# Attention output projection in three fp32r parts, with head outputs and weight split into high and low, and less scratch for GpSimd's DMAs

## The reference

```python
q = (x @ Wq.T + bq); k = (context @ Wk.T + bk); v = (context @ Wv.T + bv)   # to 16 heads of 32
attn = softmax(einsum('bhnd,bhmd->bhnm', q, k) * scale, axis=-1)
out = einsum('bhnm,bhmd->bhnd', attn, v)      # heads side by side again: (n, 512)
return out @ Wo.T + bo
```

## Time and profile before

| | |
|---|---|
| time, median of 3 runs | 2181.3 us (2181.11 to 2185.82) |
| profiled execution, its own time | 2182.54 us |
| its span | 2180.8 us |
| granted TensorE clock, mean | 0.965 |
| busy, share of the span | PE 92%, PEld 60%, DVE 65%, ACT 56%, POOL 18% |
| instructions | 39849 |

### The profile page before, as it was taken

One profiled execution on the slowest core, in us unless ns is written; L12 is line 12 of the kernel. 1 busy time (PEld: TensorE's weight loads), 2 busy tenths in 40 slices (PEclk: granted clock), 3 DMA queues, 4 the chain that ended last, 5 costly groups with the idle time before them and its releaser, 6 DMA issues. The chain is left out here.

```text
span 2180.8 us, 39849 instructions
## 1 busy us (share of the span) xinstructions
PE 2004.3 (92%) x13356; PEld 1317.6 (60%) x13356; DVE 1413.9 (65%) x2811; ACT 1223.4 (56%) x3068; POOL 389.6 (18%) x595
## 2 busy tenths in 40 slices
PE   4799999999999999858999999999999999689978
PEld 3576767666766676544555555555655564278843
DVE  6778786868686868526556565656565655266428
ACT  3353535353535353317878787777777777246514
POOL 1010101010101010230221212122222222100006
PEclk9899999999999999978999999999999999889989
DMA  4304040303030303232323232424342322261165
GB/s 162 84 18 118 17 119 20 117 21 113 17 115 21 114 16 98 81 120 65 110 76 112 74 113 73 118 80 117 79 117 79 102 75 69 77 218 59 58 228 216
DMA packets 117216, 200.94 MB, mean 92 GB/s; under 512 B 22944, under 2 KB 40352, under 8 KB 117024
## 3 DMA queue, kind: packets, MB, share of 16 engines
q1 hardware_dynamic: 107808, 179.46, 27.0%
q0 software_dynamic: 9216, 18.89, 3.4%
HBM read 117.53 MB, written 29.88 MB: 68 GB/s over the span
## 5 line engine op out<-in xcount | busy, mean ns | idle before, releaser
L1555 ACT ACTIVATE a_shared<-a_shared,a_mx 128x512 f32<-128x512 f32 x512 | 340.6, 668 | 51.0 <-DVE a_mx L1603 50.9
L1548 ACT ACTIVATE a_probs<-a_scores 128x512 f32<-128x512 f32 x512 | 291.7, 602 | 111.2 <-PE a_scores L1706 109.0
L1603 DVE TENSOR_REDUCE a_mx<-a_shared 128x1 f32<-128x512 f32 x512 | 318.3, 681 | 29.8 <-PE a_shared L1690 29.2
L901 PE MATMUL m_proj<-m_xt_hi,link 128*128 128x512 f32 x576 | 242.3, 421 | 38.4 <-DVE m_xt_lo L635 25.8
L1706 PE MATMUL a_scores<-a_qs,a_ks 98*128 98x512 f32 x512 | 217.8, 434 | 21.1 <-ACT a_probs L1548 17.3
L1690 PE MATMUL a_shared<-a_ks,a_qs 96*128 96x512 f32 x512 | 220.6, 443 | 14.4 <-ACT a_shared L1555 11.4
L902 PE MATMUL m_proj<-m_xt_lo,link 128*128 128x512 f32 x576 | 231.0, 401 | 0.0
L903 PE MATMUL m_proj<-m_xt_hi,link 128*128 128x512 f32 x576 | 229.8, 399 | 0.0
L1043 PE MATMUL m_outp<-m_wout,m_g 128*128 128x512 f32 x512 | 224.8, 597 | 2.7 <-issue 2.7
L1664 PE MATMUL a_shared<-link 128*128 128x512 f32 x768 | 190.9, 402 | 18.6 <-POOL a_ks L1495 15.7
L625 DVE SCALAR_TENSOR_TENSOR m_acc<-m_proj,m_cw,m_acc 128x511 f32<-128x511 f32 (+2 forms) x216 | 160.8, 748 | 64.1 <-ACT m_acc L452 58.3
(11 more groups left out here) (242 smaller groups left out, 3336.1 us busy)
## 6 DMA issues: line engine op xcount, KB each, us to landing
m_dec<-step_decay SPq DMA_DIRECT2D x64, 256.0 KB, 4.2
a_qs<-link SPq DMA_DIRECT2D x256, 64.0 KB, 2.3
m_ce<-run_decay SPq DMA_DIRECT2D x128, 112.0 KB, 3.2
a_ks<-a_k_hi POOLq DMA_DIRECT2D x192, 64.0 KB, 2.6
e_x<-x SPq DMA_DIRECT2D x11, 1024.0 KB, 5.2
m_xt_in<-x_t_in SPq DMA_DIRECT2D x8, 1024.0 KB, 7.8
m_x_tok<-x_in SPq DMA_DIRECT2D x8, 1024.0 KB, 6.0
x<-m_x_tok SPq DMA_DIRECT2D x32, 256.0 KB, 2.2
```

The lines of the kernel that those rows point to most:

```text
L901: pe.matmul(bank[:, :], wh, xt_hi[:, k, :], start=(k == 0), stop=False)
L1548: act.activation(probs[:, n % 2, h, :], scores[t.score_bank(n, h)][:, :], ACT.Exp, scale=-1.0).then_inc(exp_ready, 1)
L1555: act.activation(scored[:, :], scored[:, :], ACT.Exp, scale=-1.0, bias=mx[:, i % 2, j, h:h + 1], accum_out=den[:, i, j, h:h + 1]).then_inc ...
L1603: dve.tensor_reduce(mx[:, i % 2, j, h:h + 1], bank(what)[:, :], AX.X, ALU.min).then_inc(mx_ready, 1)
```

## The change

The output projection is made like the other projections: `o` and the weight are each held as a high and a low part in fp32r, and `out` is 12 fp32r matmuls in place of 4 fp32 matmuls. The weight is loaded into `x_tok`, which is free at that time, and split by 8 DVE instructions (`wo`) at the start of the part "first", that is ahead of the first unit of the first sequence. The head outputs are split right after each `norm` by a new step `osplit` of 2 DVE instructions (the second waits for the first); `norm` writes to `inv_rows` in place. The bias of v moves from the copy of v, which becomes a plain copy, to `osplit`, as one value per partition. The scratch that holds the descriptors of GpSimd's DMAs is set to 2048. In the third stage three small tensors are allocated in another place and three semaphores are shared with earlier ones that are done.

```diff
         if u == 0:
             put("norm", group, 0, 0, d)
+            put("osplit", group, 0, 0, d)
...
-            "first": [(step, d) for step, d in steps if d >= 0],
+            "first": [(("wo", i, 0, 0), 0) for i in range(KT)] + [(step, d) for step, d in steps if d >= 0],
...
-                for i in range(2):
-                    sp.dma_start(brow[:, i, :], b_row[i].partition_broadcast(P)).then_inc(small_in, 16)
-                sp.dma_start(w_o[:, :, :], woT.rearrange("(k p) n -> p k n", p=P)).then_inc(small_in, 16)
+                sp.dma_start(brow[:, :], b_row[1].partition_broadcast(P)).then_inc(small_in, 16)
+                sp.dma_start(bvcol[:, :], b_row[0]).then_inc(small_in, 16)
+                sp.dma_start(x_tok[:, :, :], woT.rearrange("(k p) n -> p k n", p=P)).then_inc(small_in, 16)
...
                 elif kind == "load":
+                    if t.first():
+                        sp.wait_ge(wo_s, 2 * KT)
...
-                    dve.tensor_tensor(v[:, i, :], bank(what)[:, :], brow[:, 0, :], ALU.add).then_inc(v_ready, 1)
+                    dve.tensor_copy(v[:, i, :], bank(what)[:, :]).then_inc(v_ready, 1)
...
+                    dve.tensor_tensor(inv_rows[:, :], o_bank[:, :], inv_rows[:, :], ALU.mult).then_inc(o_ready, 1)
+                elif kind == "osplit":
                     if i == 0 and not t.first():
                         dve.wait_ge(out_done, t.at(TT, 0))
-                    dve.tensor_tensor(o[:, i, :], o_bank[:, :], inv_rows[:, :], ALU.mult).then_inc(o_ready, 1)
+                    dve.wait_ge(o_ready, t.at(KT, i + 1))
+                    dve.tensor_scalar(o_hi[:, i, :], inv_rows[:, :], bvcol[:, i:i + 1], None, ALU.add
+                                      ).then_inc(o_split, 1)
+                    dve.wait_ge(o_split, t.at(2 * KT, 2 * i + 1))
+                    dve.scalar_tensor_tensor(out=o_lo[:, i, :], in0=inv_rows[:, :], scalar=bvcol[:, i:i + 1],
+                                             in1=o_hi[:, i, :].bitcast(F32), op0=ALU.add, op1=ALU.subtract
+                                             ).then_inc(o_split, 1)
+                elif kind == "wo":
+                    dve.wait_ge(small_in, N_SMALL)
+                    dve.tensor_copy(wo_hi[:, i, :], x_tok[:, i, :]).then_inc(wo_s, 1)
+                    dve.wait_ge(wo_s, 2 * i + 1)
+                    dve.tensor_tensor(wo_lo[:, i, :], x_tok[:, i, :], wo_hi[:, i, :].bitcast(F32), ALU.subtract
+                                      ).then_inc(wo_s, 1)
...
                 elif kind == "out":
                     if i == 0:
-                        pe.wait_ge(o_ready, t.at(KT, KT))
+                        pe.wait_ge(wo_s, 2 * KT)
+                        pe.wait_ge(o_split, t.at(2 * KT, 2 * KT))
                     take(part, what, t)
                     for k in range(KT):
-                        ins = pe.matmul(bank(what)[:, :], o[:, k, tile], w_o[:, k, :], start=(k == 0),
-                                        stop=(k == KT - 1))
+                        for n, (op, wp) in enumerate(((o_hi, wo_hi), (o_hi, wo_lo), (o_lo, wo_hi))):
+                            ins = pe.matmul(bank(what)[:, :], op[:, k, tile], wp[:, k, :], start=(k == n == 0),
+                                            stop=(k == KT - 1 and n == 2))
...
-    nc = bacc.Bacc("TRN2", target_bir_lowering=False, num_devices=1)
+    nc = bacc.Bacc("TRN2", target_bir_lowering=False, num_devices=1, dynamic_dma_scratch_size=2048)
```

More of the change, by code:

```diff
@@ L1310, in attention_stage @@
         w_lo = {n: kept[i][1] for i, n in enumerate(names)}
-        w_o = sb("wo", [P, KT, DM])
-        brow = sb("brow", [P, 2, DM])
+        wo_hi = sb("wo_hi", [P, KT, DM], F32R)
+        wo_lo = sb("wo_lo", [P, KT, DM], F32R)
+        brow = sb("brow", [P, DM])
+        bvcol = sb("bvcol", [P, KT])
         ident = sb("ident", [P, P])
@@ L1332, in attention_stage @@
         inv_rows = sb("inv_rows", [P, SEQ])
-        o = sb("o", [P, KT, SEQ])
+        o_hi = sb("o_hi", [P, KT, SEQ], F32R)
+        o_lo = sb("o_lo", [P, KT, SEQ], F32R)
         stats = sb("stats", [P, TT, 6])
@@ L1345, in attention_stage @@
         small_in = sem("small_in")
+        wo_s = sem("wo_s")
+        o_split = sem("o_split")
         const = sem("const")
@@ L1511, in step @@
                     pool.tensor_tensor(x_tok[:, :, :], x_tok[:, :, :],
-                                       brow[:, 1, :].unsqueeze(1).to_broadcast([P, TT, DM]), ALU.add).then_inc(xb_ready, 1)
+                                       brow[:, :].unsqueeze(1).to_broadcast([P, TT, DM]), ALU.add).then_inc(xb_ready, 1)
                 elif kind == "out":
@@ L1592, in step @@
                     dve.wait_ge(v_done, t.at(TT, i + 1))
-                    if part == "start" and i == 0:
-                        dve.wait_ge(small_in, N_SMALL)
                     if not t.first():
                         dve.wait_ge(av_done, t.at(UNITS, i + 1 - TT))
-                    dve.tensor_tensor(v[:, i, :], bank(what)[:, :], brow[:, 0, :], ALU.add).then_inc(v_ready, 1)
+                    dve.tensor_copy(v[:, i, :], bank(what)[:, :]).then_inc(v_ready, 1)
                 elif kind == "p1":
@@ L1781, in moe_stage @@
         x2_scale = sb("x2_scale", [P, 3, n_seq * TT])
-        stats = sb("stats", [P, TT, 6])
-        mv = sb("mv", [P, n_seq, TT, 2])
-        norm = sb("norm", [P, n_seq, 4, TT])
         ss = sb("ss", [P, 3, TT])
@@ L1797, in moe_stage @@
         hs = sb("hs", [P, 2, P])
+        stats = sb("stats", [P, TT, 6])
+        mv = sb("mv", [P, n_seq, TT, 2])
+        norm = sb("norm", [P, n_seq, 4, TT])
         xnt = work[:, 0:2048].rearrange("p (k n) -> p k n", k=KT)
@@ L1857, in moe_stage @@
         c_in = [sem("c_in0"), sem("c_in1")]
-        var_ready = sem("var_ready")
-        nmr_ready = sem("nmr_ready")
-        mv_ready = sem("mv_ready")
         x3_out = sem("x3_out")
@@ L1866, in moe_stage @@
         rstd_ready, rstd_had = rn_ready, n_seq
+        mv_ready, mv_had = ssb_ready, n_seq
+        var_ready, var_had = dn_ready, n_seq
+        nmr_ready, nmr_had = mc_ready, n_seq
         N_SMALL = 4
@@ L1989, in _ @@
                     mean, var = mv[:, b, t, 0:1], mv[:, b, t, 1:2]
-                    pool.wait_ge(mv_ready, n)
+                    pool.wait_ge(mv_ready, mv_had + n)
                     pool.tensor_tensor(norm[:, b, 0, t:t + 1], var, eps_zero[:, 0:1], ALU.add).then_inc(var_ready, 1)
                     pool.tensor_tensor(norm[:, b, 1, t:t + 1], eps_zero[:, 1:2], mean, ALU.subtract)
-                    pool.wait_ge(var_ready, n)
+                    pool.wait_ge(var_ready, var_had + n)
                     pool.tensor_tensor(norm[:, b, 2, t:t + 1], norm[:, b, 0, t:t + 1], neg_half[:, 0:1],
@@ L2072, in _ @@
                 for t in range(TT):
-                    act.wait_ge(nmr_ready, b * TT + t + 1)
+                    act.wait_ge(nmr_ready, nmr_had + b * TT + t + 1)
                     act.activation(residual[b][:, t, :], residual[b][:, t, :], ACT.Identity,
@@ L2381, in lay_out @@
         "b_qk": np.stack([i[t + "bq"], i[t + "bk"]]).reshape(2, KT, P).transpose(2, 0, 1),
-        "bv": i[t + "bv"], "bo": i[t + "bo"],
+        "bv": i[t + "bv"].reshape(KT, P).T, "bo": i[t + "bo"],
         "gamma": i[f + "ln_gamma"], "beta": i[f + "ln_beta"], "mu": i[f + "mu"].reshape(DM, SLOTS),
```

## The result

| | before | after |
|---|---|---|
| time, median of 6 runs | 2181.2 us (2179.97 to 2185.82) | 2197.9 us (2195.42 to 2199.93) |
| profiled execution, its own time | 2182.54 us | 2197.65 us |
| its span | 2180.8 us | 2195.9 us |
| granted TensorE clock, mean | 0.965 | 0.955 |

The change makes the kernel slower: ratio 1.0066, 95% interval 1.0054 to 1.0078, some 14 us (the two medians lie 16.7 us apart, which the interval, up to 17.0 us, still holds). The time lies above the predicted range (2167.5 to 2192).

A forecast was written before the change was run, and what follows sets the result against it. PE and ACT were taken to hold each other up in turn, at a given PE speed. The terms +3.4, +1.0, -3.8, -0.6 and -1.4 summed to -1.4 us, from 2181.3 to 2179.9 us; the 8-in-10 range was 2167.5 to 2192.

The forecast's parts named there:

- `wo`: Start of the part "first": copies and subtractions of some 4.6 us on DVE, costing +3.4 us (2.5 to 5) once.
- six sequences: The sequences between first and last: gate gain less unit 12's loss, 6 x (-1.1 + 0.5), given as -3.8 us.
- last sequence to unit 12: Last sequence: the gate gives 1.1 us and unit 12 takes some, -0.6 us.
- end, with the third stage: Very end: DVE splits, then four outputs run with nothing beside them, 1.3 - 2.77 = -1.4 us; third stage unmoved.
- the clock: Rival, chance 0.04: in the first sequence `wo` leaves PE little to do, and slower matmuls add 2 to 4 us.
- GpSimd's bias: Last sequence, unit 12: a split waiting for GpSimd's bias add is late by up to 2 us, left in the range.
- the outputs pass on 2.46 us: Behind the outputs of each sequence: of 2.77 us saved on PE, 0.36 + 1.43 + 0.67 = 2.46 us goes on.
- the gate in unit 4: Between `norm` and `xt_lo`, which PE waits for: the split costs 1.3 us there, leaving 1.1 of 2.46.
- units 8 and 0: Splits there are covered by idle time and cost nothing; without that cover each costs up to 0.6 us.
- Unit 12: The split there makes ACT late by 1.3 us, of which some 0.5 is passed on (0.2 to 1.3).
- the splits hidden: Rival, chance 0.15: `xt_lo` is not the gate, so all 2.46 us pass in seven sequences; -14 us, 2167.
- The splits set the pace: Rival, chance 0.17: three of four norms in a sequence pass on 1.3 us in full; +13 us, 2194.

The follow-up runs named there:

- e3: Kernel after with the four `wo` steps moved into the part start, ahead of DVE's last copies of q and k; 2192.74 us, ratio 1.0036 to before.
- e8: Kernel after with x loaded in unit 10 in place of 9, putting GpSimd's last bias add behind unit 12's split; 2197.54 us, ratio 1.0064 to before.
- e4: Kernel after with the splits of groups 0, 1 and 2 moved one unit later (units 5, 9, 13); 2176.87 us, ratio 0.996 to before.
- e1: Kernel after with each output again as 4 plain fp32 matmuls on the high parts, everything else kept; 2222.24 us, ratio 1.0174 to before.
- e5: Kernel before with only the scratch for GpSimd's DMAs set to 2048; 2184.71 us, ratio 1.001 to before.
- e7: Kernel after with matmuls that nothing reads put where the added DVE work leaves PE idle; 2193.41 us, ratio 1.0043 to before.
- e9: Kernel after with only group 0's split moved, from the gate in unit 4 to unit 5; 2183.89 us, ratio 0.9998 to before.
- e10: Kernel after with only the splits of groups 1 and 2 moved, from units 8 and 12 to 9 and 13; 2188.45 us, ratio 1.0025 to before.
- e11: Kernel after with `wo` in the part start and all four splits a unit later; 2167.33 us, ratio 0.9932 to before.
- e6: Kernel after with `wo` in the part start and the splits of groups 0 to 2 a unit later; 2167.45 us, ratio 0.993 to before.

## Why the prediction was wrong

The sum held where it priced work and waits, and failed where a wait changed the speed of what follows. Its terms against the traced execution, which took 2197.65 us, close to the median:

| term | predicted, us | measured without the added falls of the clock and the bias | added by these |
|---|---|---|---|
| first stage | 0 | +1.2 | |
| `wo` | +3.4 | +3.1 | +3.7 clock |
| first sequence | +1.0 | +0.8 (from e3) | |
| six sequences | -3.8 | -3.1 | +6.2 clock |
| last sequence to unit 12 | -0.6 | 0.0 (from e8, with its clock) | +2.7 bias and clock |
| end, with the third stage | -1.4 | -1.0 | +1.6 clock |
| sum | -1.4 | +1.0 | +14.2 |

- **The step that failed** is the clock. I had it as a rival of 0.04, only in the first sequence, for 2 to 4 us, and wrote that its case would end inside the range. The sum and all other rivals took PE's speed as given. The runs showed instead that PE's clock falls behind the waits that the new DVE work makes: at `wo` (3.7 us), in four more falls in the six sequences, two of them behind the gate (4 x 1.55 = 6.2), and at the end (1.6). There PE waits 2.24 us for the last split, and the first output takes 4.6 us in place of 3.0:

```profile
1890.61 0.47 PE L1756 MATMUL a_shared<-a_wo_hi,a_o_hi 128*128 128x512 f32 x1 [2.24 <-DVE a_o_lo L1637]
...
1891.25 0.63 PE L1756 MATMUL a_shared<-a_wo_hi,a_o_lo 128*128 128x512 f32 x1
```

- Together 11.5 of the 15.1 us. The cause is shown for the head and the gate. The other two of the four falls in the six sequences come at the end of unit 11, where the change adds no wait of its own worth more than 0.2 us. A fall there stands in the kernel before (sequence 6) and in e4, where the splits are late, and none in e8, where every split is in its place. So it is not shown that the change brings them; these 3.1 us may be scatter between executions, and why some sequences show a fall and others none stays open at both places.
- **GpSimd's bias** was seen, and left out of the sum as "late by up to 2 us". It held the split for 1.70, so its size was right and its place in the sum was not; the 2.7 us of the table are this and the lower clock of the last sequence, which no run takes apart. The row of it was there, 4.57 us long from 1844.40, and the split of unit 12 had to fall into it. I expected the two-input half of the split to be held; it was the one-input half.
- **The first stage** is not changed, and starts of attention's first score tile lie from 1013.7 to 1017.8 us over the thirteen traces of this study, whose first stage is the same code. The +1.2 is of that scatter.
- **Right**: the prices of output, split and `wo`; that the outputs pass on 2.46 us (2.44 measured by units 2, 3 and 4; e1 has 2.4); the gate in unit 4 with 1.3 (1.31 in the sequences without a fall); units 8 and 0 covered; the net of a sequence at full clock (-0.5 on average once the falls are taken off, where -0.6 was predicted; from output 0 to output 0 it is -0.6 in two of the three stretches without a fall and -0.1 in the third); scratch at next to nothing (e5). When GpSimd's DMAs wait for scratch, and for what, no run shows beyond the pauses of e5. Unit 12 passes on 0.14 and not 0.5; 0.3 more comes up only behind unit 14. ACT's idle behind outputs 1 and 2 shrinks by 1.2 and not 1.4 us (2.69 in sequence 3, 3.86 before), and its gap at the start of "first" is 2.97 us. One sum was written wrong: 6 x (-1.1 + 0.5) is -3.6 and not -3.8, or -4.0 with the 1.16 that stands behind the 1.1. Nothing hangs on it.
- **The rivals**: the splits hidden did not happen, but is what e4 makes of them. The splits set the pace (2194) had the nearest time for another reason; e4 rules its mechanism out.

## What to carry to other kernels

A wait put on a busy TensorE is not priced by its length alone: where the granted clock falls behind it, the matmuls that follow run at half speed. Here that came behind a wait of 1.3 us in 12 of 20 sequences and cost some 1.5 us each time. So work of another engine that PE waits for goes to the place where that engine's results are wanted last, not to where its input is ready: the same 48 instructions cost 1.1% of this kernel behind `norm` and nothing a unit later. And before DVE work is put beside a long GpSimd instruction on SBUF, look where the two fall in the last iteration, which has its own timing.

## What the runs showed of the hardware

- A wait of PE of 1.32 us, in a stretch in which PE was busy 2.02 of 3.40 us, was followed by the granted clock at 0.50. Over five kernels such a fall followed that wait in 12 of 20 sequences, and a wait of 1.05 us in the same place in 1 of 10; without the split the wait there was at most 0.35 us and no fall followed in 42 sequences; with matmuls that nothing reads in that place the clock stayed at 1.00 in six of six.
- A DVE TENSOR_SCALAR of 128x512 fp32 with one SBUF input, begun beside a running GpSimd TENSOR_TENSOR on SBUF, ended 0.28 to 0.29 us behind it in seven traces (2.02 to 4.53 us in place of 0.49: after, e1, e3, e7, e9, e10, e11), and with the same distance where it began near its end (0.94 us in e4, 0.68 in e6, 1.27 in e8), while `norm` with one input in PSUM and one in SBUF took its 0.69 us beside the same GpSimd instruction.
- With the scratch of GpSimd's DMAs at 2048, GpSimd paused for 0.55 to 0.63 us once in every 36 DMAs (e5 and the kernel after, seven times each); in the kernel before it never did in 288.
